# GINE edge stages of a four-layer graph network: GpSimd issues its gathers without a clear of 1024 words after each group

## The reference

```python
for l in range(3):
    e = edge_attr @ W_lin[l] + b_lin[l]
    msg = relu(x[src] + e)
    agg = segment_sum(msg, dst, num_segments=n)
    h = relu((x + agg) @ W1[l] + b1[l]) @ W2[l] + b2[l]
    x = relu(batchnorm(h) * gamma[l] + beta[l])
```

## Time and profile before

| | us |
|---|---|
| median of 3 runs | 4524.12 (4523.55 to 4528.85) |
| profiled execution, own time | 4522.14 |
| its span in the trace | 4520.3 |
| granted PE clock, mean | 0.797 of full |
| PE busy | 3424.3 (76%) |
| DVE busy | 2652.9 (59%) |
| POOL busy | 2825.8 (63%) |

### The profile page before, as it was taken

One profiled execution on the slowest core, in us unless ns is written; L12 is line 12 of the kernel. 1 busy time (PEld: TensorE's weight loads), 2 busy tenths in 40 slices (PEclk: granted clock), 3 DMA queues, 4 the chain that ended last, 5 costly groups with the idle time before them and its releaser, 6 DMA issues. The chain is left out here.

```text
span 4520.3 us, 91957 instructions
## 1 busy us (share of the span) xinstructions
PE 3424.3 (76%) x20700; PEld 2666.3 (59%) x20793; DVE 2652.9 (59%) x6184; ACT 1615.5 (36%) x3137; POOL 2825.8 (63%) x2944
## 2 busy tenths in 40 slices
PE   6999999967777755555655555555556799999997
PEld 3777777745555534444444444444444688898894
DVE  5888888866666653333333333333334788888885
ACT  3666666645555531111211111211113333333334
POOL 4555555537777758888678888588884444444440
PEclk7999999979999965555555555655556899999998
DMA  3333333313223212222122222122221333333330
GB/s 113 92 100 100 99 99 100 101 48 80 80 80 80 79 50 59 58 58 59 47 68 59 58 59 59 55 60 58 59 59 48 108 110 110 106 110 109 106 101 15
DMA packets 293253, 349.80 MB, mean 77 GB/s; under 512 B 63537, under 2 KB 236756, under 8 KB 292916
## 3 DMA queue, kind: packets, MB, share of 16 engines
q0 software_dynamic: 98528, 229.12, 17.9%
q1 hardware_dynamic: 140481, 92.05, 7.5%
q10 hardware_dynamic: 54162, 27.77, 2.2%
HBM read 332.61 MB, written 16.07 MB: 77 GB/s over the span
## 5 line engine op out<-in xcount | busy, mean ns | idle before, releaser
L988 POOL DMA_INDIRECT gath<-source_rows_narrow,gine_idx x1176 | 1136.7, 967 | 386.2 <-issue 316.1
L1038 DVE TENSOR_TENSOR vs<-psum,gath 128x512 f32<-128x512 f32 x366 | 253.1, 692 | 1027.7 <-SPq L973 954.0
L1004 PE MATMUL psum<-gine_lin,ea 32*128 32x128 f32 x2928 | 288.4, 483 | 749.3 <-DVE vs L1038 721.7
L1144 POOL DMA_INDIRECT gath<-source_rows,idx_all x416 | 430.3, 1034 | 509.5 <-DVE vs L1265 352.8
L760 POOL DMA_INDIRECT gath<-source_rows,idx_all x488 | 465.1, 953 | 377.2 <-PE psum L807 262.3
L1004 PEld LDWEIGHTS psum<-gine_lin,ea 32*128 32x128 f32 x2928 | 183.8, 297 | 849.9 <-DVE vs L1038 778.7
L760 POOL DMA_INDIRECT gath<-source_rows_narrow,idx_all x488 | 462.8, 948 | 206.1 <-issue 136.6
L790 PE MATMUL psum<-lk,att_b 128*128 128x512 f32 x732 | 375.2, 619 | 113.8 <-DVE lk L885 113.2
L1068 ACT ACTIVATE pm<-vs 128x512 f32<-128x512 f32 x186 | 117.2, 630 | 811.1 <-DVE vs L1038 806.6
L807 PEld LDWEIGHTS psum<-gath,pt 128*128 128x128 f32 x2928 | 365.1, 192 | 36.8 <-DVE zsum L918 1.8
L1013 PE MATMUL psum<-hot,pm 128*128 128x128 f32 x1488 | 363.4, 421 | 20.4 <-ACT pm L1068 19.4
(11 more groups left out here) (243 smaller groups left out, 6412.2 us busy)
## 6 DMA issues: line engine op xcount, KB each, us to landing
rel<-rel_rows SPq DMA_DIRECT2D x244, 128.0 KB
ea<-in_edge_attr_tiles SPq DMA_DIRECT2D x416, 64.0 KB
ea<-in_edge_attr ACTq DMA_DIRECT2D x366, 64.0 KB
gath<-source_rows_narrow,gine_idx POOLq DMA_INDIRECT x1176
gath<-source_rows,idx_all POOLq DMA_INDIRECT x904
rel<-quad_rel_rows SPq DMA_DIRECT2D x104, 128.0 KB
gath<-source_rows_narrow,idx_all POOLq DMA_INDIRECT x488
source_rows<-ACC SPq DMA_DIRECT2D x12, 512.0 KB, 2.9
```

The lines of the kernel that those rows point to most:

```text
L988: pool.indirect_dma_start(out=ring[:, g % RING, j, :], out_offset=None, in_=table1, in_offset=bass.IndirectOffsetOnAxis(ap=gine_idx[:, g, ...
L1004: last = e.matmul(E[:, j, :], ea[rows, s, :], gine_lin[rows, layer, :], start=True, stop=True)
L1038: v.tensor_tensor(vs[:, s, :].rearrange("p (j d) -> p j d", j=SUBS), E, ring[:, bass.ds(slot, 1), :, :].rearrange("p a j d -> p (a j) d"), ...
L1144: pool.indirect_dma_start(out=gath[:, q % 4, j, :], out_offset=None, in_=table, in_offset=bass.IndirectOffsetOnAxis(ap=quad_idx[:, q, j:j ...
```

## The change

After the four gathers of a group POOL goes straight on to the next one. The clear, the wait ahead of it and their semaphore are gone. Nothing else changes: the ring of eight slots, the four slots for one-hots, messages and sums, and the programs of the other engines stay.

```diff
-        gi_landed, gi_free, gi_paused = sem("gine_landed"), sem("gine_free"), sem("gine_paused")
+        gi_landed, gi_free = sem("gine_landed"), sem("gine_free")
...
                             pool.indirect_dma_start(
                                 out=ring[:, g % RING, j, :], out_offset=None, in_=table1,
                                 in_offset=bass.IndirectOffsetOnAxis(ap=gine_idx[:, g, j:j + 1], axis=0)).then_inc(gi_gath[g % RING], 16)
-                        wait(pool, gi_paused, layer * GROUPS + g)
-                        pool.memset(hot_t[0:1, :, :], 0.0).then_inc(gi_paused, 1)
```

## The result

| | before | after |
|---|---|---|
| median, us | 4526.49 (4 runs) | 4295.70 (4291.85 to 4296.55, 4 runs) |
| profiled execution, us | 4522.14 | 4296.55 |
| its span, us | 4520.3 | 4294.7 |
| three edge parts, first gather to end of last, us | 577.3, 574.2, 574.1 | 500.0, 501.4, 501.7 |

The ratio is 0.9491 with a 95% interval of 0.9477 to 0.9505: 230.8 us faster, 6.3 us under the 4302 of the forecast. The profiled execution became 225.6 us shorter. Of these 222.5 us went in the three edge parts (1725.5 to 1503.1); the other 3 are spread over the stages before and behind.

The account below looks back on a forecast made before the run. POOL's gather issue was taken to bound all three edge parts. From 4522.14 us profiled, less 233 for the group borders, plus 11 for delayed gathers, came 4300; plus 1.98 for the median, 4302 us, range 4283 to 4385.

Parts of the forecast that it names:

- POOL's issue is the bound: In all three edge parts POOL's gather issue rate sets the pace, 577.70, some 575 and 575.00 us; consumers starve.
- 0.80 us for each of 291 borders, 233 us: Between two groups' gathers on POOL, 1.10 us falls to 0.30; 97 borders in each of 3 layers save 233 us.
- The catches cost 11 us more: Gathers delayed by a running two-SBUF-operand DVE is_equal, behind two-item groups: 25 to 44 us against 23.5, taken as 11 more.
- the replay: One-item and two-item groups re-timed without the clear: two gathers behind a two-item group lose 0.19 and 0.42 us.
- Only an instruction already running at the gather's start catches it: A DVE is_equal begun 0.05 us before a gather stretched it to 1.45 us; begun 0.02 after, 0.95.
- the prediction's remark that a gather doesn't hold up `is_equal`: Against the skill's rule, a running gather doesn't delay DVE's is_equal: longest 694 ns, one started 0.48 us into a gather.
- Ordinary groups pass: In one-item groups the third gather starts 0.04 us ahead of is_equal, the fourth after its end; neither is delayed.
- this rival: Third gathers in ordinary groups are delayed by is_equal, up to 0.55 us each: 4385 us, or 4424; chance 0.13.
- The rest is unchanged: The nodes' parts and the 2.75 us tail behind the last gather stay; the median lies 1.98 us above the profiled execution.
- Slower by the gathers' own queue: The gathers' DMA queue can't drain one each 1.25 us, so POOL stands in each gather: 4606 us; chance 0.03.

Follow-up runs that it names:

- the two kernels without catches: The kernel before and the changed kernel, each with is_equal reading its column numbers from PSUM instead of SBUF: 4500.30 and 4267.52 us.
- the numbers in PSUM: The changed kernel with is_equal's column numbers read from PSUM instead of SBUF and two PSUM banks for the sums instead of four: 4267.52 us.
- short clear: The kernel before with its wait and clear kept, the clear cut from 1024 words to 16: 4299.88 us, ratio 0.9498.

## Why the prediction was right

- *POOL's issue is the bound.* Right. After the change DVE still waits for SP, POOL for nothing but itself, and with two gathers left out the next bound shows at 359 us an edge part.
- *0.80 us for each of 291 borders, 233 us.* Right: 232.8 us between the two kernels without catches, 0.30 to 0.31 us at the borders of the trace.
- *The catches cost 11 us more.* Right in sign and kind: 11.1 us by the excess above 0.947 us of the gathers over 0.97, 8.6 us by the busy time of all gathers, since the others came out 2 ns shorter. In the group shown the replay placed the catches within 0.03 us of where they came, and the numbers in PSUM show that the second SBUF operand is their cause. That the sum is so close to the 11 is in part luck: this was the middle of a span of 2 to 21.
- *Only an instruction already running at the gather's start catches it.* Nearly. It must be some 0.04 us ahead. Of the `is_equal` that began 0.040 us ahead or less none caught its gather, three in the kernel after; these took 0.74 to 0.76 us themselves. So the prediction's remark that a gather doesn't hold up `is_equal` fails for starts this close, by up to 0.08 us.
- *Ordinary groups pass.* Right, with little to spare: in the group shown the third gather passed by 0.09 us. Of the 150 third gathers in groups that are neither double nor right behind a double one, nine were caught. The margin was some 0.04 us wider than the replay's 0.04, since an `is_equal` that little ahead still lets the gather pass. With `is_equal` half a microsecond earlier 111 of the 150 were caught, so the 0.13 for this rival was not too much.
- *The rest is unchanged.* Nearly; 3 us went outside the edge parts. The forecast for the profiled execution was 4300 and it took 4296.55, 3.6 less. The forecast added 1.98 for the median, and the median came 0.85 below the profiled execution instead: 3.6 + 2.0 + 0.85 is, but for rounding, the 6.3 us between 4302 and 4295.70. The difference of the medians, 230.8, is larger than the profiled 225.6 because the profiled execution before lay 4.4 us under its median.
- *Slower by the gathers' own queue.* Out: with the numbers in PSUM 392 gathers follow one another at 489.1/392 = 1.25 us, and none is stretched.

The version with the numbers in PSUM beats both kernels: 4267.52 us, ratio 0.9430 (0.9414 to 0.9446).

## What to carry to other kernels

Where an engine issues without ever waiting for anybody, each microsecond between two of its instructions is worth its full price times its count, until the next bound. A short instruction in between is free only as long as it fits beside the preparation of the next one. Before a pacing engine is sped up, lay its new start times against the instructions of the other engines that can stop it: the change of phase is a term of the sum, of either sign. The cure here was to take an operand out of SBUF: it removed every collision, in both phases, for 27 to 28 us. Moving the instruction earlier made more of them; moving it later was not tried.

## What the runs showed of the hardware

- A gather is stopped by a DVE instruction with two SBUF operands only if this one began some 0.04 us ahead of it: the smallest lead of one that stopped a gather is 0.041 us in the kernel after and 0.042 before, the largest of one that did not is 0.043 us (short clear). The gather then ends 0.82 us after that instruction does (0.815 to 0.823 us in the kernel after; 2317.00 + 1.12 - 2317.30 in the group shown).
- With a smaller lead, or just behind the gather's start, DVE is the one held up: in the kernel after the three `is_equal` that began 0.016 to 0.040 us ahead of a gather took 740 to 762 ns, two begun 0.03 us behind its start 697 ns, and all five ended 0.72 us after that start. From 0.04 us on behind it nothing shows on either side. So neither engine is held for as long as the gather lasts. The median of the 366 `is_equal` is 685 to 687 ns.
- With one of the two operands in PSUM neither of the two happens: leads of 0.004 to 0.116 us left the gather at 947 ns at most and `is_equal` at 693.
- The clear is not stopped: in the kernel before 11 of the 294 clears began while `is_equal` was running, and each took 942 ns as the others do.
- Two clears of 1024 words in a row start 0.89 us apart though each shows 0.94, so the duration of this clear overstates by some 0.05 us what a second one adds. A clear of 16 words takes 0.10 us.
- PE's granted clock stayed near half (0.51 to 0.58) in edge parts where PE was busy two thirds of the time, up from 57%; the denser stream didn't lift it.
